# The weights' stage moved into the first normalisation, which runs chunk by chunk, and a new layout of the normalised tokens in DRAM

## What is computed

```python
# _ln_c: normalise each token (pixel) over its 128 channels
x = x + _L0_conv_ref(_ln_c(x), w_reduce, b_reduce, w_span, b_span)   # involution, 7x7, dilation 2
t = _to_tokens(x)
t = t + _L0_ffn_ref(_ln_t(t), sigma, phi, M_u, M_phi_plus, M_phi_minus, log_weights, gumbel)
...
# _L0_conv_ref
red = einsum('bchw,oc->bohw', x, w_reduce) + b_reduce      # 32 reduced channels
ker = einsum('bohw,ko->bkhw', red, w_span) + b_span        # 8 groups x 49 taps for every pixel
out = einsum('bgckhw,bgkhw->bgchw', patches, ker)          # patches: 7x7 windows of the padded x
# _L0_ffn_ref: four candidates, mixed by weights
y_soft = softmax(log_weights + gumbel); y_hard = one_hot(argmax(y_soft))
weights = y_hard - y_soft + y_soft
out = sum_i weights[i] * (spectral(sigma, M_phi_plus[i], M_phi_minus[i]) + ar(M_u[i]))
```

## Time and profile before

| what | value |
|---|---|
| time, median of 3 runs | 2880.88 us (2879.06 to 2890.47) |
| the profiled execution, its own time | 2882.68 us |
| span of its trace | 2880.8 us |
| PE / DVE / ACT / POOL busy | 81% / 52% / 46% / 12% |
| granted TensorE clock, mean | 0.913 of full speed |

### The profile page before, as it was taken

One profiled execution on the slowest core, in us unless ns is written; L12 is line 12 of the kernel. 1 busy time (PEld: TensorE's weight loads), 2 busy tenths in 40 slices (PEclk: granted clock), 3 DMA queues, 4 the chain that ended last, 5 costly groups with the idle time before them and its releaser, 6 DMA issues. The chain is left out here.

```text
span 2880.8 us, 78979 instructions
## 1 busy us (share of the span) xinstructions
PE 2343.8 (81%) x34528; PEld 1790.1 (62%) x34528; DVE 1492.2 (52%) x3491; ACT 1312.5 (46%) x2623; POOL 356.3 (12%) x682
## 2 busy tenths in 40 slices
PE   0455799958439999999999999999795984899898
PEld 0234788834128888888888888888532751344444
DVE  6342343447305565566666556666411453476777
ACT  0463243436215665566656666666310454333332
POOL 0112111114400000000000000000012001112221
PEclk9866798979769999999999999999998787899999
DMA  6436555536551111111111111100298520000000
GB/s 202 123 114 111 98 108 105 110 129 221 152 129 43 30 29 43 45 44 45 44 45 44 40 40 45 44 23 21 68 302 307 155 67 13 9 24 21 24 24 26
DMA packets 176948, 235.04 MB, mean 82 GB/s; under 512 B 32396, under 2 KB 134953, under 8 KB 173097
## 3 DMA queue, kind: packets, MB, share of 16 engines
q1 hardware_dynamic: 143749, 133.43, 16.7%
q0 software_dynamic: 32864, 96.64, 12.4%
HBM read 141.68 MB, written 88.31 MB: 80 GB/s over the span
## 5 line engine op out<-in xcount | busy, mean ns | idle before, releaser
L961 DVE COPY spc_g<-spc_pz 128x512 f32<-128x512 f32 x1024 | 629.5, 682 | 314.4 <-PE spc_pz L857 314.3
L931 ACT ACTIVATE spc_g<-spc_pz 128x512 f32<-128x512 f32 x1024 | 549.7, 610 | 291.6 <-PE spc_pz L857 291.1
L857 PE MATMUL spc_pz<-spc_v,spc_as 108*128 108x128 bf16 x8192 | 556.7, 220 | 20.5 <-issue 8.2
L857 PEld LDWEIGHTS spc_pz<-spc_v,spc_as 108*128 108x128 bf16 x8192 | 476.8, 98 | 108.9 <-ACT spc_g L931 31.4
L878 PE MATMUL spc_pz<-spc_g,spc_u 128*20 128x128 f32 x16384 | 467.0, 274 | 20.6 <-DVE spc_g L961 17.3
L878 PEld LDWEIGHTS spc_pz<-spc_g,spc_u 128*20 128x20 f32 x16384 | 451.0, 135 | 45.4 <-ACT spc_g L931 30.2
L1468 PE MATMUL moe_ex<-moe_ew,moe_d 128*128 128x512 f32 x512 | 250.2, 611 | 32.9 <-DVE moe_yt L1625 32.5
L842 PE MATMUL spc_pu<-spc_f,spc_s 128*128 128x256 f32 x768 | 208.6, 397 | 80.9 <-DMA spc_s<-s_sf 80.9
L1625 DVE SCALAR_TENSOR_TENSOR moe_yt<-moe_ex,moe_gb,moe_yt 128x128 f32<-128x128 f32 x768 | 209.6, 343 | 102.0 <-ACT moe_yt L1527 96.8
L501 DVE SCALAR_TENSOR_TENSOR inv_xo<-inv_pa,inv_mask,inv_xo 128x256 f32<-128x256 f32 x256 | 123.6, 484 | 222.5 <-PE inv_pa L459 162.1
L479 ACT ACTIVATE inv_b<-inv_pb 112x1024 f32<-112x1024 f32 x128 | 125.1, 1021 | 222.3 <-PE inv_pb L438 222.3
(11 more groups left out here) (205 smaller groups left out, 2251.2 us busy)
## 6 DMA issues: line engine op xcount, KB each, us to landing
s_yd<-spc_yo SPq DMA_DIRECT2D x128, 160.0 KB
s_sf<-fwd_so SPq DMA_DIRECT2D x16, 1024.0 KB, 6.5
spc_s<-s_sf POOLq DMA_DIRECT2D x32, 512.0 KB, 6.3
ivs_y<-s_yd POOLq DMA_DIRECT2D x32, 512.0 KB, 5.1
s_td<-ivs_to SPq DMA_DIRECT2D x32, 512.0 KB, 4.4
ln_t<-s_td SPq DMA_DIRECT2D x32, 512.0 KB, 3.8
inv_x<-s_xn SPq DMA_DIRECT2D x88, 112.0 KB
inv_x<-s_xn POOLq DMA_DIRECT2D x88, 112.0 KB, 7.9
```

Of the source, the lines that this page charges most:

```text
L857: m = pe.matmul(pz[:, (p + 2) % 3, e // 4, 2 * FT * (e % 4):2 * FT * (e % 4) + 2 * FT], AS[:, x, 8 * p + e, :], V[:, k, x, :, FT * t:FT * ...
L931: act.activation(g_out(p, 0), g_in(p, 0), ACT.Copy).then_inc(ga, 1)
L961: v.tensor_copy(g_out(p, 1), g_in(p, 1)).then_inc(gd, 1)
```

## The change

`prepare` is gone as a stage, and its work is done inside `normalise_in`. The parts are:

- **Weights inside.** SP issues the loads of the matrices between the loads of x. DVE runs the weights' operations at fixed steps of its loop (`weights(s)`). The second sign's combination and split run on POOL. POOL also writes the zeros and all six stores of `AS`.
- **Single chunks.** The stage is written out as 37 steps. In step `s` an engine works on chunk `s` with its first operation, on chunk `s-1` with its next one, and so on. PSUM is used as three pairs of buffers (`px`, `pn`, `pr`).
- **Loads of x** are issued by SP, and wait for the chunk four earlier to be turned.
- **Layout.** `XN` is [row, x, w, b, y, c] in place of [row, x, y, w, b, c]. A chunk is stored with 2 DMAs of 1 KB rows in place of 4 DMAs of 512-byte rows. A tile of the involution is read in rows of 4 KB in place of 2 KB, and the first loads of a tile and band are 2 DMAs of 448 KB (`tile_in`) in place of 8 DMAs of 112 KB. SP issues the first `residual` after two tiles in place of after all four.

```diff
-def prepare(nc, I, S):
...
+        def steps(body):
+            for s in range(NQ + 5):
+                body(s)
...
         @block.gpsimd
+            def combine():
+                step(pool.tensor_tensor(a1, acc[:, 0, :], acc[:, 1, :], ALU.subtract))
+                step(pool.tensor_tensor(a1.rearrange("p (k e) -> p k e", k=KF), a1.rearrange("p (k e) -> p k e", k=KF),
+                                        sv, ALU.mult))
+                step(pool.tensor_copy(ab[:, 1, KF * C:KF * C + C], au[:, 1, :]))
+                step(pool.tensor_copy(ab[:, 1, KF * C + C:], au[:, 2, :]))
...
+            step(pool.memset(eps[:], EPS_C))
+            step(pool.memset(zero[:], 0.0))
+            pool.wait_ge(xn_ready, 4)
+            for side in (0, HP - PADH):
+                pool.dma_start(S["XN"][side:side + PADH].rearrange("h x w b y c -> (h x w b y c)").rearrange("(p m) -> p m", m=2048),
+                               zero[0:PADH * HP, :]).then_inc(out_done, 16)
+                for k in range(PADH):
+                    pool.dma_start(S["XN"][PADH:PADH + HW, :, side + k].rearrange("h x b y c -> (h x) (b y c)"),
+                                   zero[0:2 * HW, 0:2 * NB * C]).then_inc(out_done, 16)
...
+            pool.wait_ge(mats_used, 4)
+            combine()
+            split3(pool, ab[:, 1], tmp[:, 1], parts[:, 1, 0], parts[:, 1, 1], parts[:, 1, 2], step)
+            pool.sem_inc(parts_ready[1], 1)
+            store_parts(0)
+            store_parts(1)
+            pool.wait_ge(out_done, 256)
         @block.sync
...
+            for q in range(NQ):
+                b, n = divmod(q, NCH)
+                if q + D < NQ:
+                    load_x(q + D)
+                sp.wait_ge(xn_ready, q + 1)
+                for v in range(NT // 2):
+                    r0 = PADH + 4 * n + 2 * v
+                    sp.dma_start(S["XN"][r0:r0 + 2, :, PADH:PADH + HW, b].rearrange("u x w y c -> (u x) w (y c)"),
+                                 xn[:, q % D, 2 * v:2 * v + 2].rearrange("p y c -> p (y c)")).then_inc(outs[q % D], 16)
+                if q in (1, 6, 9):
+                    load_mats((1, 6, 9).index(q) + 1)
...
         @block.vector
+            def weights(s):
+                if s == 2:
+                    mixture()
+                elif s in (5, 8, 11, 14):
+                    add_mats((5, 8, 11, 14).index(s))
+                elif s == 10:
+                    inverse_weights()
+                elif s in (16, 18):
+                    combine(s // 2 - 8)
+                elif s in (20, 22, 24, 26):
+                    split(s // 2 - 10)
...
+            def body(s):
+                if live(s):
+                    statistics(s)
+                if live(s - 1):
+                    scales(s - 1)
+                if live(s - 5):
+                    take(s - 5)
+                weights(s)
...
+        def tile_in(eng, band, tw):
+            for x in range(2):
+                src = S["XN"][16 * band:16 * band + 8, x, 8 * tw:8 * tw + ROW].rearrange("r w b y c -> r w (b y c)")
+                eng.dma_start(X[:, tw, band, x].rearrange("p b y c -> p (b y c)"), src).then_inc(x_in[band][tw], 16)
...
-            for tw in range(4):
-                for row in range(8):
-                    rows_in(sp, 0, 0, row, tw)
-            for n in range(3):
-                residual(n)
+            tile_in(sp, 0, 0)
+            tile_in(sp, 0, 1)
+            residual(0)
+            tile_in(sp, 0, 2)
+            tile_in(sp, 0, 3)
+            residual(1)
+            residual(2)
...
-        "XN": dram("s_xn", [HP, 2, 2, HP, NB, C]),
+        "XN": dram("s_xn", [HP, 2, HP, NB, 2, C]),
```

More of the change, by code:

```diff
@@ new lines, in split @@
+            def split(k):
+                if k == 0:
+                    step(v.tensor_copy(parts[:, 0, 0], ab[:, 0]))
+                elif k == 1:
+                    step(v.tensor_tensor(tmp[:, 0], ab[:, 0], parts[:, 0, 0], ALU.subtract))
+                elif k == 2:
+                    step(v.tensor_copy(parts[:, 0, 1], tmp[:, 0]))
+                else:
+                    step(v.tensor_tensor(parts[:, 0, 2], tmp[:, 0], parts[:, 0, 1], ALU.subtract))
+                    v.sem_inc(parts_ready[0], 1)
@@ L349, in involution @@
+            v.wait_ge(const_in, 48)
+            steps(body)
 def involution(nc, I, S, R):
@@ L409, in _ @@
             for tw in range(4):
-                for row in range(8):
-                    rows_in(pool, 1, 0, row, tw)
+                tile_in(pool, 1, tw)
             for n in range(NPH):
```

434 lines of the change are left out of this document (209 added, 225 removed).

## The result

The changed kernel takes 2843.85 us (median of 4 runs, 2834.71 to 2860.17) where the kernel before took 2882.06 beside it: a ratio of 0.987, 95% interval 0.983 to 0.991. It is faster, by 38 us and not by the 93 us (68 + 25) that I forecast, and 18 us above the upper end of the range. The profiled execution took 2834.71 us, of which 2832.9 are span.

The account below looks back on a forecast made before the run. Normalisation was taken as a chain through four engines, none full; DMA limited the involution's start, PE the rest. 2882.7 - 68 (first stage) - 25 (involution's start) - 1.8 (median) gave 2788 us, range 2762 to 2826.

Parts of the forecast that it names:

- Part 1: DVE in the merged first stage: chunks at 2.6 us plus 34.5 us of weights' work, 134 us if no transfer is late.
- my case: Whole kernel: involution starts at 165 to 190 us and gains 20 to 26 us, 2776 to 2808 us, chance 0.54.
- Part 2: Token stores in the merged stage: four DMA engines carry 146 to 172 us, middle 152; SP ends near 160 us.
- the largest risk: Merged stage: x late behind matrices and stores, added as a few us of idle and not read off a row.
- Part 3: POOL's half of the weights in the merged stage: 28 us, ending near 108 us, costing nothing by itself.
- Rival B: Steps 15 to 26: DVE and POOL hold each other up, 15 to 25 us added, 2803 to 2813 us; chance 0.22.
- Part 4: Stores of parts at the merged stage's end: 16.5 us, 8 us not covered, involution's start placed at 176 us.
- Part 5: Involution's start: larger tile DMAs at 200 to 280 GB/s, third apply_b after 33.4 us, gain 26 us, taken as 25.
- Part 6: Steady part of the involution and later stages: bound by PE, no change in time.
- A: Merged stage: transfers cost less than thought, the stage ends at 145 us, 2757 us in all; chance 0.13.
- C: Merged stage: POOL slow with many short rows; 2817 us in the middle (chance 0.06), up to 2907 us (0.03).
- D: Whole kernel: no effect, because another resource refills the time; chance 0.02.

Follow-up runs that it names:

- e16: Changed kernel with both signs on DVE, zero and parts stores spread out, token stores on eight engines, measured again: 2794.03 us, .966 of the kernel before.
- e1: Changed kernel with token stores as 8x16 rows of 1 KB (eight engines) in place of 4x32: 2851.58 us, .9872 of the kernel before.
- e7: Changed kernel with both signs' combination and split on DVE, no arithmetic on GpSimd: 2844.33 us, .9886 of the kernel before.
- e11: Changed kernel with both signs on DVE, each zero store at its own chunk and each part stored after its split: 2832.53 us, .9834 of before.
- e6: Changed kernel with GpSimd's own sign's parts stored first, ahead of DVE's: 2848.44 us, .9881 of the kernel before.
- e4: Kernel before with only the new XN layout and changed involution, without the merged stage: 2861.81 us, .9907 of the kernel before.
- e15: Changed kernel measured and profiled again, unchanged: 2842.18 us, .9842 of the kernel before.
- e10: Changed kernel's first stage with the layout and involution of the kernel before: 2880.11 us, .9959 of the kernel before.
- e5: Changed kernel with GpSimd's zero stores issued behind its half of the weights, not at 27 us: 2842.9 us, .9848 of the kernel before.
- e8: Changed kernel with 16 dependent small loads between the first stage and the involution: 2884.13 us, 1.0008 of the kernel before.
- e14: Kernel before with 16 dependent small loads between its first stage and the involution: 2919.59 us, 1.0125 of the kernel before.
- e9: Changed kernel with 43 dependent small loads ahead of everything else: 2933.02 us, 1.0186 of the kernel before.
- e17: Kernel before with only TensorE's loop of the normalisation stage written out: 2891.12 us, 1.0035 of the kernel before.

## Why the prediction was wrong, and where right

The profiled execution was forecast at 2789.7 us and took 2834.7. The 45.0 us are: the start of the involution 31.0 (207.0 for 176), its first three `apply_b` 2.5, the steady part 17.8, the rest -6.3. Between the profiled execution and the median lie another 9.1 us, where I had subtracted 1.8.

- *Part 1, DVE* was right but for the lock: 32 chunks at 2.6 us and 34.5 us for the weights are 117.7 us, and the 126.2 us measured are 113.1 without the 13.1 that it was locked out. From 106 to 163 us it waited only once, for 0.55 us. With the waits cut to 24.4 us (e16) the stage ends at 164.6, at the lower end of my case.
- *Part 2 is the step that failed*: "transfers lead, narrowly, and the two partly add". I summed bytes on four engines (152 us) and let that sum run beside DVE's 134. The runs showed a chain, in which a load of x that is only four chunks ahead is late behind 3.4 MB of zeros, 2.3 MB of matrices or 3.5 MB of parts: 64.1 us of waits come on top of DVE's 126.2. Halving the stores' share of the four engines took off 9.8 us (e1), and moving no byte, only spreading them, 16.0 (e7 to e11). I had named this lateness as the largest risk and left it at "a few us of idle". The sum was loose besides: 160 + 8 + 3 is 171, and the 5 us up to the 176 stand for no term; with the 78 us that I called the stores' best case the four engines' sum would start at 138 and not at 146.
- *Part 3, GpSimd's half*: 23.9 us for 28, right in size. "It costs nothing by itself" was wrong. Rival B, which I gave 0.22, was the right mechanism, at 13.1 us for 15 to 25, and e7 shows that the half is worth nothing. Its sign, L378 taking us while GpSimd works, came.
- *Part 4, the parts*: I took their 16.5 us as hidden but for 8. The size was right, the DMA share is near 1 for some 16 us (166 to 182); but they stood ahead of the last two loads of x, which I had not asked about, and the waits behind them are 20.8 us. e6, which moves half of the parts away, leaves 10.8 of it and adds 7.0 elsewhere.
- *Part 5* was right: 36.9 us for 33.4, a gain of 22.5 for 25, at 208 GB/s for the tiles (200 to 280 forecast). The 3.5 us are one wait of 3.29 us for a tile, L524 for `inv_x`, which I had given as a sign of being wrong: tiles aren't quite hidden. e4 has the part by itself: 21.9 us.
- *Part 6, "Nothing"*, was wrong by 17.8 us in the profile, and by more in the second profile (34.4 in e15). The bound is PE, as I said; but I took PE's clock from one profile as if it belonged to the involution. Here it went with the stage in front. What in the new stage lowers it is **open**: the layout (e4, e10), GpSimd's half (e7), the place of zeros and parts (e5, e11), the moment of the start (e8, e14) and rest ahead (e9) are each excluded as the cause by itself; TensorE's written-out code may be some 10 of e10's 28 us by the times, and no profile shows how. The new order itself, a chunk at a time with the weights between, was never tried with a looped TensorE, and stays as a rival.
- *Rivals* A, C and D did not come. A's 145 us for the stage were out of reach even for the best kernel. C's 205 for slow rows is near the measured 207.0 by chance: the parts moved at the old pace.

## What to carry to other kernels

Where a stage is fed by loads a few chunks ahead, don't stop at adding up the bytes of an engine: list what can stand in front of each load, block by block, and compare with the time that the look-ahead covers. Here a block larger than that was paid at every place tried, and what helped was to cut it up and spread it; only then did the bytes on the four engines show in full. Work moved from DVE to GpSimd beside DVE operations with two SBUF inputs or beside its copies should be counted as no gain until a trace shows that those operations keep their length. When a stage that PE bounds has unchanged instructions and another length, multiply length by granted clock first: here that product held within 3% over twenty profiles, and it turned a puzzle about waits into one about the clock.

## What the hardware showed that I had not expected

- The spread between runs of one kernel goes with TensorE's clock: 17 runs of the kernel before go from 2869.99 us at a mean granted clock of .913 to 2903.83 at .906, and the changed kernel from 2827.97 at .911 to 2854.52 at .898. One profile of the changed kernel had .84 in the steady involution and the next .80, 16.5 us apart.
- Beside a block on GpSimd's queue SyncE was held up in the issue itself: 10.84 us for two stores (1.1 otherwise), 10.97 us for one load of x (0.5 otherwise).
- Writing out TensorE's loop in one stage, with the same work, cost 0.35% (0.08 to 0.62; e17).
